# Attention of a Flamingo layer: scores on 32-row tiles of TensorE, the router turned round and one step later, transposed probabilities copied by ScalarE and VectorE in turn

## The reference

```python
x = x + tanh(g_xattn[0]) * L0_xattn(layernorm(x), ctx, ctx, Wq, bq, Wk, bk, Wv, bv, Wo, bo)
#   q, k, v projected, 16 heads of 32, 77 context tokens; softmax(q k^T * scale) v; then Wo, bo
x = x + tanh(g_ffn[0]) * L0_ffn(layernorm(x), router_w, router_b, ...)
#   logits = layernorm(x) @ router_w + router_b     (8 experts, the best 2 of them are used)
x = x + tanh(g_xattn[1]) * L1_xattn(layernorm(x), ctx)
x = x + tanh(g_ffn[1]) * L1_ffn(layernorm(x), w1, conv, w2)
```

## Time and profile before

| | |
|---|---|
| median of 3 runs | 1919.27 us (1912.75 to 1922.49) |
| the profiled execution | 1918.68 us |
| its span in the trace | 1917.2 us |
| busy share of the span | PE 86%, DVE 59%, ACT 41%, POOL 31% |
| granted PE clock, mean | 0.904 of full |

### The profile page before, as it was taken

One profiled execution on the slowest core, in us unless ns is written; L12 is line 12 of the kernel. 1 busy time (PEld: TensorE's weight loads), 2 busy tenths in 40 slices (PEclk: granted clock), 3 DMA queues, 4 the chain that ended last, 5 costly groups with the idle time before them and its releaser, 6 DMA issues. The chain is left out here.

```text
span 1917.2 us, 26044 instructions
## 1 busy us (share of the span) xinstructions
PE 1653.6 (86%) x8636; PEld 1304.5 (68%) x8636; DVE 1137.7 (59%) x1946; ACT 794.9 (41%) x1417; POOL 588.0 (31%) x541
## 2 busy tenths in 40 slices
PE   7599999999866999998999999837674889999997
PEld 5578888788745888886778888624343666666664
DVE  3587878878745344532223333258875777777775
ACT  2243433434313422222334443325563556566653
POOL 0133323333212444464331000065513243344440
PEclk9798989889967999999999999957666899999999
DMA  3112122121129889984443333287743111111102
GB/s 124 44 45 88 55 77 88 44 88 55 67 74 351 286 304 316 321 282 138 162 139 107 107 108 106 94 303 287 256 148 110 44 44 66 66 66 38 51 23 88
DMA packets 108196, 252.02 MB, mean 131 GB/s; under 512 B 15027, under 2 KB 15027, under 8 KB 103912
## 3 DMA queue, kind: packets, MB, share of 16 engines
q1 hardware_dynamic: 65272, 121.98, 19.0%
q0 software_dynamic: 17056, 67.12, 9.7%
q10 hardware_dynamic: 25808, 62.14, 9.2%
HBM read 147.13 MB, written 101.97 MB: 130 GB/s over the span
## 5 line engine op out<-in xcount | busy, mean ns | idle before, releaser
L1275 PE MATMUL e_u_ps<-e_w,e_xeT 128*128 128x512 f32 x1596 | 393.1, 398 | 10.8 <-DVE e_xeT L1180 10.8
L1275 PEld LDWEIGHTS e_u_ps<-e_w,e_xeT 128*128 128x128 f32 x1596 | 293.1, 189 | 73.3 <-DVE e_w L1229 8.9
L1988 PE MATMUL b_f_ps<-b_xdT,w1q 128*128 128x512 f32 x1024 | 254.1, 404 | 11.5 <-DVE b_h L1893 9.4
L1988 PEld LDWEIGHTS b_f_ps<-b_xdT,w1q 128*128 128x128 f32 x1024 | 191.4, 190 | 64.8 <-DVE b_h L1893 18.3
L1826 POOL TENSOR_TENSOR b_h<-b_h,b_srow 128x512 f32<-128x512 f32 x112 | 143.6, 1342 | 245.9 <-ACT b_srow L1847 245.9
L1286 PE MATMUL e_y_ps<-e_w,e_hT 128*128 128x512 f32 x798 | 209.9, 405 | 4.3 <-DVE e_hT L1211 2.8
L1286 PEld LDWEIGHTS e_y_ps<-e_w,e_hT 128*128 128x128 f32 x798 | 143.3, 190 | 31.0 <-issue 4.0
L1854 ACT ACTIVATE b_h<-b_f_ps,cb,cw 128x512 f32<-128x512 f32 x128 | 104.2, 814 | 124.5 <-PE b_f_ps L1988 124.3
L1890 DVE SCALAR_TENSOR_TENSOR b_h<-b_f_ps,cw,b_h 128x511 f32<-128x511 f32 x128 | 95.9, 749 | 85.9 <-ACT b_h L1854 85.7
L490 ACT ACTIVATE pT<-t_ps 77x512 f32<-77x512 f32 x128 | 71.9, 590 | 119.0 <-PE t_ps L691 119.0
L465 POOL TENSOR_TENSOR prob<-prob,ri 128x1232 f32<-128x1232 f32 x32 | 74.9, 2341 | 115.3 <-DVE ri L572 115.3
(11 more groups left out here) (221 smaller groups left out, 2869.1 us busy)
## 6 DMA issues: line engine op xcount, KB each, us to landing
e_xe<-slots_in_scratch SPq DMA_DIRECT2D x69, 256.0 KB, 2.6
experts_out_scratch<-e_ye ACTq DMA_DIRECT2D x69, 256.0 KB, 2.0
xin<-in_x SPq DMA_DIRECT2D x16, 512.0 KB, 3.8
xres<-in_x SPq DMA_DIRECT2D x16, 512.0 KB, 4.5
x_scratch<-x SPq DMA_DIRECT2D x32, 256.0 KB, 2.1
xn_scratch<-xn SPq DMA_DIRECT2D x32, 256.0 KB, 2.1
e_xe<-xn_scratch SPq DMA_DIRECT2D x32, 256.0 KB, 4.2
e_fraw<-in_w1T ACTq DMA_DIRECT2D x8, 1024.0 KB, 8.3
```

Source lines behind the costliest of these rows:

```text
L1275: mm = pe.matmul(u_ps[:, i], xeT[:, pa, k], w[:, par, pb, k * 2 * HID:(k + 1) * 2 * HID], start=(k == 0 and (pa, pb) == PASSES[0]), stop=( ...
L1988: mm = pe.matmul(f_ps[:, u % RING], w1q[:, k, m * P:(m + 1) * P], xdT[:, part, k], start=(k == 0 and part == 0), stop=(k == KD - 1 and par ...
```

## The change

1. Scores: `k_blocks` is gone, and with it its copies on ACT and DVE, and the low part of `qT` on DVE. Each head is a plain f32 matmul of its own: 32 rows of `qT` (one row tile of PE) against 32 rows of `k_all`, 77 columns; 16 of them a tile. Two row tiles alternate, each with its own bank. Heads are laid out `(i, g)` and no longer `(g, i)`.
2. `pT`: of the four copies a tile ACT makes those of `i` = 0 and 2, DVE those of `i` = 1 and 3. DVE's for `j` = 0 stand behind `softmax_sum(1)`; those for `j` = 1 stand at the head of the next step.
3. Router: `rw` (padded to 32 columns) is stationary, `x2T` moves (256 columns), four partial results land on four column tiles; ACT copies them (`rT`), and two small matmuls against `fold` add them up. All of it, with the transposes of `xn2` and their copies `x2T`, comes one step later (`late`), between other pieces of the step. One DVE instruction adds the bias for both tiles.
4. `v_batch` is gone: values are read from `v_all`. The steps are written out in full, with no hardware loop, and there is one step more at the end.

```diff
-        kbd = sb("k_blocks", [P, 2, NG, GC], FR)
-        vb = sb("v_batch", [C, D], F32)
         bq_s = sb("bq_s", [P, NG], F32)
         bo_t = sb("bo_t", [P, D], F32)
-        rw = sb("rw", [P, KD, E], F32)
+        rw = sb("rw", [P, KD, HD], F32)
+        fold = sb("fold", [P, E], F32)
...
+                sp.wait_ge(cleared, 1)
+                sp.dma_start(rw[:, :, 0:E], n.router_w).then_inc(small_in, 16)
...
-                pool.memset(kbd[:].bitcast(F32), 0.0)
+                pool.memset(rw[:], 0.0)
...
+                pool.tensor_tensor(fold[:], ident[:, 0:E], ident[:, HD:HD + E], ALU.add).then_inc(cleared, 1)
...
-        qT = sb("qT", [P, 2, 2, NG, W2], FR)
+        qT = sb("qT", [P, 2, NG, W2], F32)
...
-        def whole(eng, run):
-
-            run(-1, -1, False, False, True)
-            run(0, 0, True, False, True)
-            run(1, 0, True, True, True)
-            if B > 2:
-                with eng.Fori(1, B - 1) as b:
-                    run(b * 2, b, True, True, True, 0)
-                    run(b * 2 + 1, b, True, True, True, 1)
-            run(NSTEP - 2, B - 1, True, True, True)
-            run(NSTEP - 1, B - 1, True, True, False)
-            run(NSTEP, B, False, True, False)
...
+        def whole(run):
+            for s in range(-1, NSTEP + 2):
+                run(s, s // 2, 0 <= s < NSTEP, 1 <= s <= NSTEP, s >= 2, s < NSTEP - 1)
+        t_uses, m_uses = [], []
+        for s in range(-1, NSTEP + 2):
+            mid, back, late, front = 0 <= s < NSTEP, 1 <= s <= NSTEP, s >= 2, s < NSTEP - 1
+            t_uses += [("n", s - 2, j) for j in range(2)] * late + [("x", s + 1, j) for j in range(2)] * front
+            t_uses += [("p", s, j) for j in range(2 * HG)] * mid
+            m_uses += [("o", s - 1, 0), ("o", s - 1, 1)] * back + [("r", s - 2, 0)] * late
+            m_uses += [("w", s - 1, 0), ("w", s - 1, 1)] * back + [("l", s - 2, 0)] * late
+            m_uses += [("q", s + 1, 0), ("q", s + 1, 1)] * front
+        t_at = {u: i for i, u in enumerate(t_uses)}
+        m_at = {u: i for i, u in enumerate(m_uses)}
...
+        def last_reader(kind, s, j):
+            if kind == "p":
+                return (pa_free, pv_free)[j % 2], s * HG + j // 2 + 1
+            if kind in "rl":
+                return {"r": rt_done, "l": l_free}[kind], s + 1
+            return {"n": n_free, "x": x_free, "o": o_free, "w": w_free, "q": q_done}[kind], s * 2 + j + 1
...
+                def probs(j):
+                    for i in (0, 2):
+                        u = ("p", s, j * HG + i)
+                        act.wait_ge(t_full, t_at[u] + 1)
+                        act.activation(pT[:, i * NG:(i + 1) * NG, j * P:(j + 1) * P], quads(t_bank(*u)[0:C]),
+                                       ACT.Copy).then_inc(pa_free, 1)
...
+                if late:
+                    u = ("r", s - 2, 0)
+                    act.wait_ge(m_full, m_at[u] + 1)
+                    act.activation(rT[:], m_bank(*u)[:, 0:W2], ACT.Copy).then_inc(rt_done, 1)
...
+                def probs(s, j):
+                    for i in (1, 3):
+                        u = ("p", s, j * HG + i)
+                        dve.wait_ge(t_full, t_at[u] + 1)
+                        dve.tensor_copy(pT[:, i * NG:(i + 1) * NG, j * P:(j + 1) * P],
+                                        quads(t_bank(*u)[0:C])).then_inc(pv_free, 1)
...
+                if back:
+                    probs(s - 1, 1)
...
+                if late:
+                    for j in range(2):
+                        u = ("n", s - 2, j)
+                        dve.wait_ge(t_full, t_at[u] + 1)
+                        dve.tensor_copy(x2T[:, :, j * P:(j + 1) * P], quads(t_bank(*u))).then_inc(n_free, 1)
...
+                    norm_stats(lambda j: x1[:, j], st2, mv2, mv2_done)
+                if late:
+                    u = ("l", s - 2, 0)
+                    dve.wait_ge(m_full, m_at[u] + 1)
+                    dve.tensor_tensor(logits[:, (s - 2) * 2:(s - 1) * 2],
+                                      m_bank(*u)[:, 0:2 * E].rearrange("p (j e) -> p j e", e=E),
+                                      rb[:].unsqueeze(1).to_broadcast([P, 2, E]), ALU.add).then_inc(l_free, 1)
                 if mid:
-                    if back:
-                        x1_stats()
                     softmax_sum(1)
-                if par == 1 and front:
-                    keys(b + 1)
+                    probs(s, 0)
...
-                if par == 1 and front:
-                    keys(b + 1)
...
                 def scores(j):
-                    for g in range(NG):
-                        if g % 2 == 0 and not (isinstance(s, int) and s * 4 + 2 * j + g // 2 < 2):
-                            pe.wait_ge(s_sub, s * 4 + 2 * j + g // 2 - 1)
-                        for pa, pb in PASSES:
-                            mm = pe.matmul(s_ps[:, g, 0:GC], qT[:, par, pa, g, j * P:(j + 1) * P], kbd[:, pb, g, :],
-                                           start=((pa, pb) == PASSES[0]), stop=((pa, pb) == PASSES[-1]))
-                        if g % 2:
-                            mm.then_inc(s_full, 1)
+                    for pair in range(2):
+                        use = s * 4 + 2 * j + pair
+                        if use >= 2:
+                            pe.wait_ge(s_sub, use - 1)
+                        for g in range(NG):
+                            for i in (2 * pair, 2 * pair + 1):
+                                rows = slice(i * HD, (i + 1) * HD)
+                                mm = pe.matmul(s_ps[:, i, g * C:(g + 1) * C], qT[rows, s % 2, g, j * P:(j + 1) * P],
+                                               kc[rows, b, g, :], start=True, stop=True)
+                        mm.then_inc(s_full, 1)
...
-                                              ident[:])
+                    for i in range(HG):
+                        u = ("p", s, j * HG + i)
+                        empty(t_uses, t_at, u)
+                        for g in range(NG):
+                            mm = pe.transpose(t_bank(*u)[0:C, g * P:(g + 1) * P], prob[:, j, i * NG + g, :], ident[:])
                         mm.then_inc(t_full, 1)
...
+                if late:
+                    pe.wait_ge(xn2_done, (s - 1) * 2)
+                    for j in range(2):
+                        transposes(("n", s - 2, j), xn2[:, j])
...
+                if late:
+                    u = ("r", s - 2, 0)
+                    empty(m_uses, m_at, u)
+                    pe.wait_ge(n_free, (s - 1) * 2)
+                    for k in range(KD):
+                        mm = pe.matmul(m_bank(*u)[k * HD:(k + 1) * HD, 0:W2], rw[:, k, :], x2T[:, k, :], start=True, stop=True)
+                    mm.then_inc(m_full, 1)
...
+                if late:
+                    u = ("l", s - 2, 0)
+                    empty(m_uses, m_at, u)
+                    pe.wait_ge(rt_done, s - 1)
+                    for j in range(2):
+                        mm = pe.matmul(m_bank(*u)[:, j * E:(j + 1) * E], rT[:, j * P:(j + 1) * P], fold[:], start=True, stop=True)
+                    mm.then_inc(m_full, 1)
```

More of the change, by code:

```diff
@@ L384, in before @@
[L384 to L403, removed]
@@ L438, in _, with rstd, normalise, run @@
         def _(pool):
-            def rstd(mv_sem, count, mv, ve, rs, out_sem, tmp_count):
+            temps = [0]
+            def rstd(mv_sem, count, mv, ve, rs, out_sem):
                 pool.wait_ge(mv_sem, count)
                 pool.tensor_tensor(ve[:], mv[:, :, 1], eps[:], ALU.add).then_inc(rs_tmp, 1)
-                pool.wait_ge(rs_tmp, tmp_count)
+                temps[0] += 1
+                pool.wait_ge(rs_tmp, temps[0])
                 pool.tensor_tensor(rs[:], ve[:], half[:], ALU.pow).then_inc(out_sem, 1)
-            def run(s, b, mid, back, front, par=None):
-                par = s % 2 if par is None else par
-                tmp = before(s, 0, 1, 1)
+            def normalise(s, j):
+                pool.wait_ge(ri_done, s * 2 + j + 1)
+                pool.tensor_tensor(prob[:, j], prob[:, j], ri[:, j].unsqueeze(2).to_broadcast([P, H, C]),
+                                   ALU.mult).then_inc(p_done, 1)
+            def run(s, b, mid, back, late, front):
                 if front:
-                    rstd(mv1_done, s * 2 + 4, mv1, ve1, rs1, rs1_done, tmp + 1)
+                    rstd(mv1_done, s * 2 + 4, mv1, ve1, rs1, rs1_done)
                 if back:
@@ L500, in run @@
                 if back:
-                    for i, u in enumerate(("o0", "o1")):
-                        act.wait_ge(m_full, mb + m[u] + 1)
-                        act.activation(oT[:, 0, 2 * i:2 * i + 2], m_ps[:, m[u] % 2].rearrange("p (a b) -> p a b", b=W2),
-                                       ACT.Copy).then_inc(m_hi, 1)
-                if mid and par == 0:
-                    act.activation(vb[:], vc[:, ds(b, 1), :].rearrange("c o d -> c (o d)"), ACT.Copy).then_inc(v_done, 1)
+                    for i in range(2):
```

(23 more changed lines are left out.)

239 lines of the change are left out of this document (89 added, 150 removed).

## The result

The changed kernel took 1959.87 us (median of 4 runs, 1957.82 to 1963.12) against 1920.05 us: a ratio of 1.0215 (95% interval 1.0184 to 1.0247), slower by 2.15%. 1944 was forecast, 1895 to 2010 as the range. The profiled execution took 1960.31 us, its span 1958.8. One run of the kernel "same row tile in a row" further down (1993.77 us, granted clock 0.876 where its others had 0.889 to 0.899) fell in a slower state and is left out of its row in the table.

What follows compares the result with a forecast made beforehand. PE bound the kernel before; DVE's copies then close a PE-DVE loop of 29.2 us, with 1.5 and 1.0 for the clock 31.7 a step against 29.66. 1918.7 + 28.6 (14 steps) - 3 = 1944 us, range 1895 to 2010.

Steps and rivals of the forecast that it cites:

- the loop: Each attention step runs through PE and DVE in turn via DVE's pT copies: 29.2 us at the upper clock, 26.66 before.
- the wait ahead of the fourth group: PE idles about 2.8 us a step before the first tile's last prob transposes, until DVE's copy frees their bank.
- The clock after the first wait: PE's idle stretch ahead of wq brings the lower clock: 1.5 us a step added.
- The second stretch: Transposes, router wait and wo behind it: 1.0 us a step for the lower clock, between nothing and 1.7.
- Row tiles: Scores on PE's row tiles: 1.9 to 3.6 us a tile, nearer the first; 1.87 before.
- the two paces I named: Score records every 58 ns (side-by-side matmuls) or 113 ns (router's 128-column weight loads): 1.9 or 3.6 us a tile.
- loads in turn at the upper clock: Half of the row-tile case: weight loads follow each other without the lower clock; step 32.8 us, time 1960 us.
- PE's own work: If PE stayed the bound with equal scores, a step would be 24.7 us at the upper clock.
- Head and end: First steps: nothing gained or lost; end after step 15's scores shorter; together -3 us.
- The rival at 1909 us: Loop without the price of the clock: 29.2 us a step, 1909 us; chance 0.20.
- PE as the bound: Rival: DVE copies in time and PE stays the bound; 24.7 + 0.5 us a step, 1853 us; chance 0.10.
- row tiles as the bound: Rival: score loads follow each other and bring the lower clock, in half of the steps; 2037 us; chance 0.16.

Runs made afterwards that it cites:

- same row tile in a row: Changed kernel with the scores reordered so that neighbouring matmuls share a row tile; 1964.57 us, ratio 1.0240.
- experiment 6: Changed kernel with DVE's two x2T copies moved ahead of xn and oT, pT copies left late; 1924.61 us, ratio 1.0025.
- experiment 8: Changed kernel with all pT copies on ScalarE, x2T copies first and the next xin load ahead of the x1 and xn2 stores; 1847.61 us, ratio 0.9612.
- experiment 3: Changed kernel with 24 extra matmuls that nothing reads ahead of the first tile's fourth group of transposes; 1933.87 us, ratio 1.0069.
- experiment 4: Changed kernel with scores of one row tile first, then of the other, so that neighbours share a tile; 1964.57 us, ratio 1.0240.

## Why the prediction was right, point by point

- **The bound of before, and the loop.** Right. I had the wait ahead of the fourth group at 2.8 us, it is 2.54; DVE idle before its next copy at "about 4", it is 6.25, since `wq` is slow and `xn2` took 1.17 (most of it after POOL's `normalise`) and not 2.86. The forecast loop against one turn of it, from the end of one copy (346.58) to the end of the next (378.98), in us:

| piece | forecast, upper clock | measured |
|---|---|---|
| last group of transposes | 0.6 | 0.48 |
| `wq` | 5.84 | 7.24 |
| second tile's transposes and copies | 3.1 (its pieces add up to 3.18) | 3.39 |
| DVE from statistics to copy | 19.6 | 21.29 |
| sum | 29.2 | 32.40 |

- **The clock after the first wait.** Forecast 1.5, measured 1.4 in this turn (7.24 for 5.84), and shown apart by the filled stretch: 1.44 us a step, 1.34 of it in `wq`.
- **The second stretch.** This is the term that was too small. I put the wait ahead of the router, behind the `xn` transposes. It is ahead of the `xn` transposes, since they reuse the banks that hold `xn2`'s: those of the first tile start when the first `x2T` copy is through (332.04 + 0.69, PE at 332.86), not the second, as experiment 6 has it (through at 333.32):

```profile
332.04 1.28 DVE L584 COPY x2T<-t_ps 128x512 f32<-128x512 f32 x2
```

DVE is there on the forecast's time. PE starts these transposes 8.67 us after the second tile's transposes of `prob` in every steady turn, and about 1.1 us of them, which I had beside the wait, come after it. From there to the end of `wo` it is 7.36 us in the one turn that stays at the upper level, so `wo` would end at 16.0 and not 15.4: 0.6 us for the order. In the other twelve it is 8.59 to 10.07, on average over all thirteen 8.96: 1.6 us for the clock, where I had 1.0. In the turn of the table `wo` starts 11.56 us after the second tile's transposes (356.89 to 368.45), not 9.7. DVE, to which I gave 0.4 us of slack the other way, waits 1.83 to 1.95 us for it, and that is the 1.7 us by which DVE's piece is longer. So the step is 32.50 and not 31.7, 14 x 0.8 = 11 us of the 16 that I was low; the 5.3 us behind the attention are about the rest.

- **Row tiles.** 1.57 us for the first tile, less than the block-diagonal 1.87 and less than the 1.9 that I gave as the least with two tiles: 49 ns a record, neither of the two paces I named. The second tile's took 2.08 us in the changed kernel, about 1.6 in experiment 8. The Trainium skill's page TensorEngine Tiling (Array Packing), section Key Properties, says that different tiles load and multiply in parallel; 49 against 81 ns agrees. The Trainium skill's page TensorE: Matmul & The Clock Gate, section LDWEIGHTS, says that a load of 128 columns takes 107 ns whatever its rows; the trace doesn't agree, for records that share a tile came every 81 ns. In neither case were the scores on the path. The prediction prints 1960 us for loads in turn at the upper clock, which is the time measured, but by chance: that case needed 3.6 us of scores.
- **PE's own work.** The 24.7 us a step that PE alone would need is about right: 25.12 was measured in experiment 8, with 1.4 us of short waits left in it.
- **Head and end.** Forecast -3 in all, measured -3.5 (1.36 and 2.18 us gained).
- **The rival at 1909 us** (loop without the price of the clock) is refuted by experiment 3; PE as the bound by the first wait; row tiles as the bound by experiment 4.
- **Small slips.** The 0.6 us by which the median lies above the profiled execution is named in the sum and not added. The 1.5 for the clock was chosen between the 1.3 and 1.7 of a single stretch of before, so that it came out so near is partly luck.

## What to carry to other kernels

Work moved from a busy engine to one with room must be placed by when it is needed there: a copy of 0.6 us, put behind 3.2 us of other work in an in-order list, held up the matmuls behind it and closed a loop in which both engines waited in turn. Look for what reuses a buffer (here two banks, four groups) and ask for each wait which list the releasing instruction stands in, and behind what. An idle stretch of 2 to 3 us on TensorE cost more than itself here: count the lower clock in what follows, and once the last such stretch is gone expect more than the waits add up to.

## What the runs showed of the hardware that I had not expected

- 24 useless matmuls a step in an idle stretch of 2.5 us made the kernel 26 us faster (1.3%), 20 of them in the steps, by keeping the granted clock up in the 48 matmuls behind it.
- Plain f32 matmuls of 32 rows and 77 columns, two row tiles in turn, came every 49 ns; with neighbours on the same tile (and in the same bank) every 81 ns. Sixteen of them (32 records, the first tile of a step) took less PE time than twelve `fp32r` ones of 128 rows and 308 columns (1.57 for 1.87 us).
- Behind scores with neighbours on the same tile the clock fell in 6 of 14 steps without an idle stretch just ahead.
- With both long waits gone the clock was 1.00 over 352 us, though a quarter of that time is transposes (91.4 us of 351.7): stretches of 1 to 2 us of them between other matmuls did not lower it here.
